# Attention kernel with inverses of the sums: from a rescaling of the output to a rescaling of the probabilities

## Chip, cores and metric

One core of one Trainium2 chip. The metric is the device time of one execution in microseconds (us); less is better.

## What is computed

x has shape (4, 1024, 1024): B = 4 batches, n = 1024 rows, dim = 1024, 16 heads of d = 64. With xn the RMS-normalised and modulated x and q, k RMS-normalised per head:

```python
qkv = xn @ W_qkv
logits = jnp.einsum('bhqd,bhkd->bhqk', q, k) * d ** (-0.5)
attn = jax.nn.softmax(logits, axis=-1)
o = jnp.einsum('bhqk,bhkd->bhqd', attn, v)
x = x + o + o @ W_out
x = x + causal_depthwise_conv(x, cond, b)
```

The change touches the softmax alone: where each row of exp(logits) is divided by its sum. All products run on pairs of half-precision numbers (a value and the rest that it leaves, "high" and "low"), so that every fp32 operand X is X_hi + X_lo, and a product takes three matmuls.

## The kernel before

A preparation scales and splits the weights (to about 204 us). Then come 32 **units** u, one per batch and pair of heads, each with eight **steps** p of 128 query rows. Each engine has its own program with the same loops, written by hand, and the engines meet by semaphores; each takes its instructions in order. Units differ in what they carry besides attention: units 0 to 30 project q, k, v of the next unit (`qkv`), units 0 to 23 prepare x of a later batch (`xs`), units 8 to 31 make output products of the batch before (`outs`), and units 9 to 31 also convolve and store (`fins`).

The work of one step, for the two heads h = 0, 1:

- PE: `score` (L723, 12 matmuls of 512 columns into the PSUM tensor `scores`). It first waits until the exps of the step before have read `scores` (`exp_done`). Behind it PE does half an `attend` (L742, probabilities times values, for two steps together), parts of the projection (L774), the output product (L798, L801) or transposes (L786, L811), by the step's number.
- VectorE (DVE): `maximum` of each head (L1178) and from it the exp's bias (L1181); then the step's other work, written between: x, convolution (L1266 to L1277), `normalise` (L1209, L1213), `sums` (L1198, L1201); then `low` of each head (L1187), the low half of the probabilities: prob minus its high half.
- ScalarE (ACT): exp of each head (L888) from PSUM into `prob`, with an accumulator read that gives the row sums `total`; then `high` of each head (L896), the copy to half precision; then copies for the other work.
- POOL: low halves of other operands; a DMA transposes each head's pair (L576) for `attend`.

VectorE starts the maxima of step p+1 only behind both `low` of step p. The exp of head h waits for `low` of the same head one step earlier, which frees `prob`.

**The inverses.** Two steps give four columns of sums, a group g. `invert` on VectorE (L1236, L1239, L1241) forms 1/sum and splits it in halves. `inverses` on PE (L757) transposes them, `inverse_rows` on ScalarE (L952) reads them to `inv_row`, a matmul with the constant `sel` (L749) spreads them over 64 rows a head, `read_inverses` (L958) reads that to `inv_all`, and `scale_values` on VectorE (L1250) multiplies: oT = values * inv_all. ScalarE makes its high half (`o_high`, L965) and POOL its low half (`o_lower`, L1131). PE's next `attend` waits for the inverse row (`inv_ev`).

## Time and profile before

| what | value |
|---|---|
| median of 3 runs | 2618.7 us (2618.64 to 2621.14) |
| profiled execution | 2618.81 us |
| its span | 2616.9 us |
| PE, VectorE, ScalarE, POOL busy | 91%, 80%, 69%, 25% of the span |
| TensorE clock granted, mean | 0.958 |

The profiled execution is as long as the median run; 1.9 us of it lie outside the span. Busy PE counts an engine whose matmuls are pipelined, so 91% is no statement on how much PE could lose: that is read by stretches and from the chain of waits. Where a view shows an idle time in brackets, it names the instruction that ended it.

### The profile page before, as it was taken

Reading aid. Unit: us, or ns where it says so; the run is one execution under the profiler, and the core shown is the slowest. Engines: PE = TensorE matmul, PEld = TensorE weight load, DVE = VectorE, ACT = ScalarE, POOL = GpSimd, SP = SyncE. Lnnn points to the kernel's source line nnn. Section 1 sums busy time; section 2 is a strip of 40 time slices with the busy share of each in tenths; the row PEclk is TensorE's granted clock in tenths of the full one; section 3 lists DMA queues with packets and bytes.
Section 4 is the critical chain, followed back from the end, with each engine's and each line's share of the span. In section 5 each row is a group of like instructions: output and inputs, shape, how many; then the busy total and the mean of one; then the engine's idle time right before and its main releaser. Section 6 shows DMA issues by size and latency. Waiting matters only on the chain.

```text
span 2616.9 us, 54024 instructions
## 1 busy us (share of the span) xinstructions
PE 2372.9 (91%) x20690; PEld 1527.4 (58%) x20690; DVE 2106.6 (80%) x3360; ACT 1815.4 (69%) x2823; POOL 660.5 (25%) x460
## 2 busy tenths in 40 slices
PE   1458998888889999999999999999999999999698
PEld 0034555555556666666666666666666666666487
DVE  6757777777778888888888888888888888888845
ACT  2237777777777877777777778777777777877611
POOL 0052322223222233222233232332222222222000
PEclk8879989989989999999999999999999999999789
DMA  6877988989999999999999999999988989887841
GB/s 236 344 192 152 172 166 174 180 173 179 218 197 183 185 203 184 193 190 219 205 206 193 200 187 189 196 186 229 193 176 171 179 162 182 165 164 155 158 150 61
DMA packets 1234881, 487.07 MB, mean 186 GB/s; under 512 B 1139521, under 2 KB 1196993, under 8 KB 1232065
## 3 DMA queue, kind: packets, MB, share of 16 engines
q1 hardware_dynamic: 1234624, 483.63, 87.8%
q8 instruction: 165, 2.70, 0.4%
q14 instruction: 92, 0.75, 0.1%
HBM read 141.13 MB, written 57.18 MB: 76 GB/s over the span
## 4 chain that ended last, share of the span: by engine, by line
PE 69%; DVE 11%; issue 6%; ACT 4%; SPq 3%; DMA 1%; POOL 0%; ACTq 0%; DVEq 0%
PE proj L774 36%; PE scores L723 11%; PE values L742 10%; PE proj L798 8%; DVE neg L1178 5%; DVE p_pair L1187 4%; SPq L576 3%; ACT p_pair L896 2%; PE proj L801 1%; PE misc L811 1%; DVE bias L1181 1%; ACT prob L888 1%; PE misc L786 1%; PE values L757 1%; PE values L749 1%
## 5 line engine op out<-in xcount | busy, mean ns | idle before, releaser
L774 PE MATMUL proj<-w_sb,xn_sb 128*128 128x384 f16 x6144 | 1029.4, 327 | 33.9 <-DMA xn_sb<-p_pair 29.1
L888 ACT ACTIVATE prob<-scores,bias,l_scale 128x1024 f32<-128x1024 f32 x512 | 615.5, 1203 | 353.7 <-DVE bias L1181 336.0
L774 PEld LDWEIGHTS proj<-w_sb,xn_sb 128*128 128x128 f16 x6144 | 588.9, 98 | 434.0 <-DMA xn_sb<-p_pair 25.6
L1178 DVE TENSOR_REDUCE neg<-scores 128x1 f32<-128x1024 f32 x512 | 623.8, 1218 | 156.1 <-PE scores L723 152.3
L1187 DVE TENSOR_TENSOR p_pair<-prob,p_pair 128x1024 f16<-128x1024 f32 x512 | 614.8, 1242 | 137.6 <-ACT p_pair L896 137.6
L896 ACT ACTIVATE p_pair<-prob 128x1024 f16<-128x1024 f32 x512 | 511.0, 1049 | 0.4 <-DMA pT<-p_pair 0.4
L723 PE MATMUL scores<-stack 64*128 64x512 f16 x3072 | 391.4, 389 | 58.8 <-ACT prob L888 57.1
L742 PE MATMUL values<-pT,v_pair 128*64 128x256 f16 x6144 | 396.9, 280 | 11.0 <-DMA pT<-p_pair 6.3
L742 PEld LDWEIGHTS values<-pT,v_pair 128*64 128x64 f16 x6144 | 324.2, 112 | 93.5 <-issue 78.6
L1102 POOL TENSOR_TENSOR rs<-ms,power 128x16 f32<-128x16 f32 x64 | 185.6, 2900 | 395.6 <-DVE ms L1201 395.6
L1131 POOL TENSOR_TENSOR oT_pair<-oT,oT_pair 128x256 f16<-128x256 f32 x128 | 148.7, 1162 | 541.4 <-ACT oT_pair L965 541.4
L723 PEld LDWEIGHTS scores<-stack 64*128 64x128 f16 x3072 | 131.7, 96 | 247.6 <-ACT prob L888 68.3
L798 PE MATMUL proj<-oT_in,wo 128*128 128x256 f16 x2304 | 267.7, 273 | 0.0
L798 PEld LDWEIGHTS proj<-oT_in,wo 128*128 128x128 f16 x2304 | 220.6, 98 | 30.0
L1107 POOL TENSOR_TENSOR qk_pair<-stage,qk_pair 128x512 f16<-128x512 f32 x128 | 146.7, 1167 | 329.8 <-ACT qk_pair L919 329.8
L1277 DVE SCALAR_TENSOR_TENSOR acc<-yT,taps,acc 128x256 f32<-128x256 f32 x384 | 186.2, 485 | 13.7
L952 ACT ACTIVATE inv_row<-values 4x256 f16<-4x256 f16 x128 | 47.1, 368 | 155.4 <-PE values L757 155.3
L904 ACT ACTIVATE stage<-proj 128x384 f32<-128x384 f32 x256 | 122.4, 478 | 31.4 <-PE proj L774 31.4
L1181 DVE TENSOR_SCALAR bias<-neg,l_scale 128x1 f32<-128x1 f32 x512 | 109.6, 214 | 18.0
L1127 POOL TENSOR_TENSOR pair<-x_in,pair 128x1024 f16<-128x1024 f32 x24 | 67.9, 2831 | 209.1 <-ACT pair L946 209.1
L232 PE MATMUL ps_row<-emb_w,smallT 128*4 128x512 f32 x64 | 40.4, 791 | 74.4 <-DMA emb_w<-in_L_cond_W_emb 74.4
L977 ACT ACTIVATE yT<-proj,y_now 128x512 f32<-128x512 f32 x64 | 43.8, 685 | 86.4 <-PE proj L801 70.2
(127 smaller groups left out, 2089.3 us busy)
## 6 DMA issues: line engine op xcount, KB each, us to landing
w_sb<-w_dram SPq DMA_DIRECT2D x128, 384.0 KB, 4.1
o_dram<-oT_pair SPq DMA_DIRECT2D x128, 128.0 KB, 2.5
out<-acc SPq DMA_DIRECT2D x64, 256.0 KB, 2.7
wq_raw<-in_L_cond_W_qkv SPq DMA_DIRECT2D x8, 1536.0 KB, 10.6
w_dram<-wq_pair SPq DMA_DIRECT2D x8, 1536.0 KB, 7.4
x_in<-in_x SPq DMA_DIRECT2D x24, 512.0 KB, 4.4
oT_in<-o_dram SPq DMA_DIRECT2D x12, 1024.0 KB, 6.0
xr<-in_x SPq DMA_DIRECT2D x24, 512.0 KB, 4.1
```

What stands on the lines that cost most here:

```text
L723: last = nc.tensor.matmul(scores[:, h, n * HN:(n + 1) * HN], stack[rows_, par, i, p * P:(p + 1) * P], stack[rows_, par, j, n * HN:(n + 1) ...
L742: last = nc.tensor.matmul(values[DH * h:DH * h + DH, 0:QG].rearrange("p (a n) -> p a n", a=2), v_pair[:, par, 2 * c + h, DH * i:DH * i + D ...
L774: last = nc.tensor.matmul(proj[:, t % 2, 0:6 * DH], xn_sb[:, t, i * K + c, :], w_sb[:, c, j, :], start=(c == 0 and i == j == 0), stop=(c = ...
L798: nc.tensor.matmul(dst, const["wo"][:, c, b, m * P:(m + 1) * P], oT_[:, c, a, :], start=(c == 0 and a == b == 0), stop=False)
L888: nc.scalar.activation(prob[:, h, :], scores[:, h, :], ACT.Exp, bias=bias[:, s:s + 1], scale=const["l_scale"][:, 0:1], accum_out=total[:, ...
L896: nc.scalar.activation(p_pair[:, s % 4, 0, :], prob[:, h, :], ACT.Copy).then_inc(hi_done, 1)
L1102: nc.gpsimd.tensor_tensor(rs[:], ms[:], const["power"][:, 0:4 * KH], ALU.pow).then_inc(h_pw, 1)
L1107: last = nc.gpsimd.tensor_tensor(qk_pair[:, j, 1].rearrange("p t (h d) -> p (t h) d", d=DH), stage[:, hf, :, j * DH:(j + 1) * DH], qk_pair ...
L1131: nc.gpsimd.tensor_tensor(oT_pair[:, 1], oT[:], oT_pair[:, 0], ALU.subtract).then_inc(o_low, 1)
L1178: nc.vector.tensor_reduce(neg[:, s:s + 1], scores[:, h, :], axis=AX.X, op=ALU.max, negate=True).then_inc(max_done, 1)
L1187: nc.vector.tensor_tensor(p_pair[:, s % 4, 1, :], prob[:, h, :], p_pair[:, s % 4, 0, :], ALU.subtract).then_inc(lo_done, 1)
L1277: nc.vector.scalar_tensor_tensor(out=acc[:, m, :], in0=yT[:, m, k:k + QG], scalar=const["taps"][:, k, c:c + 1], in1=acc[:, m, :], op0=ALU. ...
```

## The change

The probabilities themselves are divided by their sum, on the way to half precision. `high` becomes a copy of prob scaled by inv = 2^15 / sum, one number per row, read from memory, and `low` becomes prob * inv - high in one scalar_tensor_tensor. So `attend` gives the finished output (times 2^15), and the transposes on PE, `inv_row`, the product with `sel`, `inv_all` and the multiplication on VectorE go. `o_high` and `o_lower` read the PSUM tensor `values` themselves; `o_lower` moves from POOL to VectorE, at the place of `scale_values`, and `o_high` moves ahead of the two `high`, at the place of `read_inverses`. PE's next `attend` now waits for `o_low` of the group before. `invert` runs for every step instead of every second: a reciprocal and a multiplication by 2^15. In units 0 to 7 the first head is inverted right behind the maxima and the second behind the step's other work; in units 8 to 31 both behind the other work. The bias moves from VectorE to ScalarE (a copy of `neg` scaled by `l_scale`), ahead of each exp; its constant shift is dropped.

```diff
@@ PE
                 if part == 0:
-                    pe.wait_ge(inv_ev, n + 1)
+                    need(pe, o_low, n)
...
                 if part == 1:
                     last.then_inc(pv_done, 1)
-                    nc.tensor.matmul(values[:, QG:2 * QG], const["sel"][:], inv_row[:],
-                                     start=True, stop=True).then_inc(all_mm, 1)
-
-            def inverses(u, g):
-                n = NG * u + g
-                pe.wait_ge(inv_done, n + 1)
-                need(pe, o_done, n)
-                for a in range(2):
-                    last = nc.tensor.transpose(inv_bank[:, a * P:(a + 1) * P], inv_pair[:, g % 2, a, :],
-                                               const["eye16"][:])
-                last.then_inc(inv_tr, 1)
@@ ScalarE
             def exponent(u, p, h, par):
                 s = 2 * p + h
+                act.wait_ge(max_done, slot(u, s) + 1)
+                nc.scalar.activation(bias[:, s:s + 1], neg[:, s:s + 1], ACT.Copy,
+                                     scale=const["l_scale"][:, 0:1]).then_inc(bias_done, 1)
+                need(act, lo_done, slot(u, s) - 1)
                 act.wait_ge(bias_done, slot(u, s) + 1)
-                need(act, lo_done, slot(u, s) - 1)
-                if s % 4 == 0:
-                    need(act, inv_done, NG * u + s // 4 - 7)
+                if h == 0:
+                    need(act, inv_done, slot(u, s) - 2 * NS + 2)
...
             def high(u, p, h):
                 s = 2 * p + h
-                act.wait_ge(exp_done, slot(u, s) + 1)
+                act.wait_ge(inv_done, slot(u, s) + 1)
                 need(act, pT_in[(s + 4) % 8], 16 * (2 * u + (s + 4) // 8))
-                nc.scalar.activation(p_pair[:, s % 4, 0, :], prob[:, h, :], ACT.Copy).then_inc(hi_done, 1)
+                nc.scalar.activation(p_pair[:, s % 4, 0, :], prob[:, h, :], ACT.Copy,
+                                     scale=inv[:, p % 2, h:h + 1]).then_inc(hi_done, 1)
...
             def o_high(u, g):
                 n = NG * u + g
-                act.wait_ge(o_done, n + 1)
+                act.wait_ge(pv_done, n + 1)
                 need(act, o_st, 16 * n)
-                nc.scalar.activation(oT_pair[:, 0], oT[:], ACT.Copy).then_inc(o_hi, 1)
+                nc.scalar.activation(oT_pair[:, 0], values[:, 0:QG], ACT.Copy,
+                                     scale=1.0 / PROB_UP).then_inc(o_hi, 1)
@@ VectorE
             def maximum(u, p, h):
...
+                need(dve, bias_done, n - NS + 1)
                 nc.vector.tensor_reduce(neg[:, s:s + 1], scores[:, h, :], axis=AX.X, op=ALU.max,
                                         negate=True).then_inc(max_done, 1)
-                dve.wait_ge(max_done, n + 1)
-                nc.vector.tensor_scalar(bias[:, s:s + 1], neg[:, s:s + 1], const["l_scale"][:, 0:1], P_SHIFT,
-                                        ALU.mult, ALU.add).then_inc(bias_done, 1)
...
-                nc.vector.tensor_tensor(p_pair[:, s % 4, 1, :], prob[:, h, :], p_pair[:, s % 4, 0, :],
-                                        ALU.subtract).then_inc(lo_done, 1)
+                nc.vector.scalar_tensor_tensor(out=p_pair[:, s % 4, 1, :], in0=prob[:, h, :],
+                                               scalar=inv[:, p % 2, h:h + 1], in1=p_pair[:, s % 4, 0, :],
+                                               op0=ALU.mult, op1=ALU.subtract).then_inc(lo_done, 1)
...
+            def invert(u, p, par, h0, h1):
+                s = 2 * p
+                dve.wait_ge(exp_done, slot(u, s) + h1)
+                nc.vector.reciprocal(inv[:, p % 2, h0:h1], total[:, par * NS + s + h0:par * NS + s + h1]
+                                     ).then_inc(inv_rc, h1 - h0)
+                dve.wait_ge(inv_rc, slot(u, s) + h1)
+                nc.vector.tensor_scalar(inv[:, p % 2, h0:h1], inv[:, p % 2, h0:h1], PROB_UP, None,
+                                        ALU.mult).then_inc(inv_done, h1 - h0)
+
+            def o_lower(u, g):
+                dve.wait_ge(o_hi, NG * u + g + 1)
+                nc.vector.scalar_tensor_tensor(out=oT_pair[:, 1], in0=values[:, 0:QG], scalar=1.0 / PROB_UP,
+                                               in1=oT_pair[:, 0], op0=ALU.mult,
+                                               op1=ALU.subtract).then_inc(o_low, 1)
...
                 for p in range(K):
                     maximum(u, p, 0)
                     maximum(u, p, 1)
+                    if not outs:
+                        invert(u, p, par, 0, 1)
...
+                    invert(u, p, par, 0 if outs else 1, 2)
                     if p % 2 == 0 and p >= 4:
-                        scale_values(u, (p - 4) // 2)
+                        o_lower(u, (p - 4) // 2)
```

Where the instructions stand, VectorE in step 7 of a unit with output work, before (in brackets the semaphores that each waits for):

```order
L1178 TENSOR_REDUCE neg<-scores 128x1 [waits qk_done]
L1181 TENSOR_SCALAR bias<-neg,l_scale 128x1 [waits max_done]
L1178 TENSOR_REDUCE neg<-scores 128x1 [waits qk_done]
L1181 TENSOR_SCALAR bias<-neg,l_scale 128x1 [waits max_done]
L1266 TENSOR_SCALAR yT<-ends,carry 128x3 [waits halo,f_st0,y_ev]
L1270 TENSOR_SCALAR acc<-yT,taps,conv_b 128x256
L1273 COPY ends<-yT 128x3 [waits halo]
L1277 SCALAR_TENSOR_TENSOR acc<-yT,taps,acc 128x256 [waits cv,halo]
L1277 SCALAR_TENSOR_TENSOR acc<-yT,taps,acc 128x256 [waits cv] x2
L1187 TENSOR_TENSOR p_pair<-prob,p_pair 128x1024 [waits hi_done] x2
L1178 TENSOR_REDUCE neg<-scores 128x1 [waits qk_done]
```

and now:

```order
L1113 TENSOR_REDUCE neg<-scores 128x1 [waits bias_done,qk_done] x2
L1193 TENSOR_SCALAR yT<-ends,carry 128x3 [waits halo,f_st0,y_ev]
L1197 TENSOR_SCALAR acc<-yT,taps,conv_b 128x256
L1200 COPY ends<-yT 128x3 [waits halo]
L1204 SCALAR_TENSOR_TENSOR acc<-yT,taps,acc 128x256 [waits cv,halo]
L1204 SCALAR_TENSOR_TENSOR acc<-yT,taps,acc 128x256 [waits cv] x2
L1167 RECIPROCAL inv<-total 128x2 [waits exp_done]
L1170 TENSOR_SCALAR inv<-inv 128x2 [waits inv_rc]
L1119 SCALAR_TENSOR_TENSOR p_pair<-prob,inv,p_pair 128x1024 [waits hi_done] x2
L1113 TENSOR_REDUCE neg<-scores 128x1 [waits bias_done,qk_done] x2
```

The biases are gone; the reciprocal and its scaling stand behind the convolution and ahead of the two subtractions.

ScalarE in the same step 7, before:

```order
L952 ACTIVATE inv_row<-values 4x256 [waits all_mm,inv_tr]
L932 ACTIVATE stack<-misc 128x2x512 [waits h_tr]
L888 ACTIVATE prob,total<-scores,bias,l_scale 128x1024 [waits lo_done,bias_done] x2
L896 ACTIVATE p_pair<-prob 128x1024 [waits pT_in2,exp_done]
L896 ACTIVATE p_pair<-prob 128x1024 [waits pT_in3,exp_done]
L932 ACTIVATE stack<-proj 128x2x512 [waits h_tr]
L977 ACTIVATE yT<-proj,y_now 128x2x256 [waits cv,op_mm,y_set]
```

and now:

```order
L903 ACTIVATE stack<-misc 128x2x512 [waits h_tr]
L852 ACTIVATE bias<-neg,l_scale 128x1 [waits max_done]
L858 ACTIVATE prob,total<-scores,bias,l_scale 128x1024 [waits inv_done,bias_done,lo_done]
L852 ACTIVATE bias<-neg,l_scale 128x1 [waits max_done]
L858 ACTIVATE prob,total<-scores,bias,l_scale 128x1024 [waits bias_done,lo_done]
L866 ACTIVATE p_pair<-prob,inv 128x1024 [waits pT_in2,inv_done]
L866 ACTIVATE p_pair<-prob,inv 128x1024 [waits pT_in3,inv_done]
L903 ACTIVATE stack<-proj 128x2x512 [waits h_tr]
```

A bias stands ahead of each exp, the second one behind the first exp; the copies to `p_pair` wait for `inv_done` instead of `exp_done`; `inv_row` is gone.

VectorE in step 6 of a unit of the first kind (u = 0 to 7), now:

```order
L1113 TENSOR_REDUCE neg<-scores 128x1 [waits bias_done,qk_done] x2
L1167 RECIPROCAL inv<-total 128x1 [waits exp_done]
L1170 TENSOR_SCALAR inv<-inv 128x1 [waits inv_rc]
L1142 TENSOR_TENSOR stage<-stage,rs 128x8x128 [waits h_pw]
L1146 TENSOR_TENSOR stage<-stage,g_qk 128x8x64 [waits h_n]
L1167 RECIPROCAL inv<-total 128x1 [waits exp_done]
L1170 TENSOR_SCALAR inv<-inv 128x1 [waits inv_rc]
L1175 SCALAR_TENSOR_TENSOR oT_pair<-values,oT_pair 128x256 [waits o_hi]
L1119 SCALAR_TENSOR_TENSOR p_pair<-prob,inv,p_pair 128x1024 [waits hi_done] x2
```

The first head's inversion stands ahead of `normalise` (the two operations on `stage`), the second one behind it.

## Rows read from the trace of the kernel before

**Rows 1.** Page, part 1: busy time, share of the span, instructions

```profile
PE   2372.9 (91%) x20690; PEld 1527.4 (58%) x20690; DVE 2106.6 (80%) x3360; ACT 1815.4 (69%) x2823; POOL 660.5 (25%) x460
```

**Rows 2.** Windows: stretch, its length, busy us by engine, PEclk, DMA

```profile
471.50:542.20 70.70, 61.66 (x526) 36.45 (x528) 53.88 (x77) 52.21 (x83) 20.16 (x14) 0.91 0.87 172
...
1627.00:1698.60 71.60, 71.49 (x646) 46.85 (x647) 62.87 (x102) 56.10 (x89) 20.99 (x14) 1.00 0.96 199
```

**Rows 3.** Timeline, PE: first scores of units 8 and 31

```profile
764.10 2.03 PE L723 MATMUL scores<-stack 64*128 64x512 f16 x12
...
2415.04 1.47 PE L723 MATMUL scores<-stack 64*128 64x512 f16 x12
```

**Rows 4.** Chain of waits, units 20 and 21: start, length in us, what

```profile
1638.49 0.20 PE values L757 x2
...
1649.47 0.21 PE values L749
...
1685.21 1.45 PE scores L723 x12
...
1698.59 1.47 PE scores L723 x11
```

**Rows 5.** Timeline, DVE and ACT, step 7 of unit 19: start, length

```profile
1622.82 1.22 DVE L1178 TENSOR_REDUCE neg<-scores 128x1 f32<-128x1024 f32 x1
...
1624.32 1.20 ACT L888 ACTIVATE prob<-scores,bias,l_scale 128x1024 f32<-128x1024 f32 x1 [1.22 <-DVE bias L1181]
...
1625.70 1.20 ACT L888 ACTIVATE prob<-scores,bias,l_scale 128x1024 f32<-128x1024 f32 x1
...
1626.23 1.53 DVE L1277 SCALAR_TENSOR_TENSOR acc<-yT,taps,acc 128x256 f32<-128x256 f32 x3
...
1626.89 1.99 ACT L896 ACTIVATE p_pair<-prob 128x1024 f16<-128x1024 f32 x2
...
1627.97 2.36 DVE L1187 TENSOR_TENSOR p_pair<-prob,p_pair 128x1024 f16<-128x1024 f32 x2 [0.21 <-ACT p_pair L896]
...
1630.25 1.22 DVE L1178 TENSOR_REDUCE neg<-scores 128x1 f32<-128x1024 f32 x1
```

**Rows 6.** Groups by line and form: busy us, mean ns of one, idle before

```profile
L896 ACT ACTIVATE p_pair<-prob 128x1024 f16<-128x1024 f32 x512 | 511.0, 1049 | 0.4 <-DMA pT<-p_pair 0.4
...
L888 ACT ACTIVATION_READ_ACCUMULATOR prob<-scores,bias,l_scale 128x1 f32 x512 | 98.6, 193 | 0.0
...
L1209 DVE TENSOR_TENSOR stage<-stage,rs 128x1024 f32<-128x1024 f32 x64 | 78.0, 1218 | 6.0 <-POOL rs L1102 6.0
...
L919 ACT ACTIVATE qk_pair<-stage 128x512 f16<-128x512 f32 x128 | 73.5, 626 | 15.0 <-DVE stage L1213 15.0
...
L952 ACT ACTIVATE inv_row<-values 4x256 f16<-4x256 f16 x128 | 47.1, 368 | 155.4 <-PE values L757 155.3
...
L1236 DVE RECIPROCAL inv<-total 128x4 f32<-128x4 f32 x128 | 21.6, 169 | 0.0
...
L1224 DVE SCALAR_TENSOR_TENSOR pT<-pT,msx,rows 128x1024 f32<-128x1024 f32 x8 | 10.3, 1285 | 10.0 <-POOL msx L1122 10.0
...
L287 DVE SCALAR_TENSOR_TENSOR wo<-wo_raw,wo_top,wo 128x1024 f16<-128x1024 f32 x8 | 9.7, 1281 | 1.3 <-ACT wo L209 1.3
...
L209 ACT ACTIVATE wo<-wo_raw,wo_top 128x1024 f16<-128x1024 f32 x8 | 8.4, 1135 | 26.5 <-DVE wo_top L283 26.5
```

**Rows 7.** Timeline, units 19 and 20: step 5, and step 0's x

```profile
1604.94 1.22 DVE L1178 TENSOR_REDUCE neg<-scores 128x1 f32<-128x1024 f32 x1 [1.63 <-PE scores L723]
...
1607.36 1.20 ACT L888 ACTIVATE prob<-scores,bias,l_scale 128x1024 f32<-128x1024 f32 x1
...
1637.95 1.69 DVE L1224 SCALAR_TENSOR_TENSOR x_in<-x_in,msx,rows 128x1024 f32<-128x1024 f32 x1
```

**Rows 8.** Timeline, PE: waits in units of the first and second kind

```profile
542.18 2.74 PE L723 MATMUL scores<-stack 64*128 64x512 f16 x12 [4.32 <-ACT prob L888]
...
1275.41 4.07 PE L774 MATMUL proj<-w_sb,xn_sb 128*128 128x384 f16 x24 [3.01 <-DMA w_sb<-w_dram]
```

103 lines of the change are left out of this document (11 added, 92 removed).

## The prediction

> **What bounds the kernel now.** The page's first part says TensorE at 91% of the span, VectorE at 80% [rows 1]. That is an average; the stretches say more. The program has 32 units (u = 0 to 31). In a unit of the second kind (u = 8 to 31, with output work) PE is busy for 71.49 of 71.6 us, over the length of one of the first kind (u = 0 to 7) only for 61.66 of 70.7, partly at the lower clock [rows 2]. The 23 units 8 to 30 run from 764.10 to 2415.04, 71.8 us each [rows 3].
>
> The chain of waits through unit 20 shows who holds whom [rows 4]. From step 0 to step 5 it stays on PE, and the transposes of the inverses (0.20) and the product with sel (0.21) lie on it. At step 6's scores (1685.21) it leaves PE and runs through VectorE and ScalarE until the next unit's scores at 1698.59. So two things are nearly level in steps 6 and 7: PE's own work, which is unbroken there, and a ring of VectorE and ScalarE. The reader has to price that ring, not PE's share.
>
> The ring in step 7, its times counted in us from its first maximum at 1622.82 [rows 5]: first exp at +1.50, second exp at +2.88, first half-precision copy (L896) at +4.07, first subtraction (L1187) at +5.15, next step's first maximum at +7.43. VectorE takes its instructions in order, so the next maximum cannot pass the two subtractions; nothing else in the ring needs PE. In steps 0 to 5 PE's work takes 9 to 10 us a step and hides the ring.
>
> **What the change takes from PE.** Eight groups of instructions per unit, four of 0.20 and four of 0.21 us on the chain [rows 4]: 1.65 us. PE alone would need 71.55 - 1.65 = 69.9 us for a unit.
>
> **What it does to the ring.** Four edges change in every step.
> (a) The bias is made on ScalarE. The first costs there what it did on VectorE plus about 0.07. The second now stands behind the first exp and its accumulator read, no longer beside them. Its size, 128x1 with a scale read from memory, is not in the trace. Ends: 0.19, the accumulator read, and 0.37, a 4x256 copy [rows 6]. The copies of 1024 and of 512 columns (L896 1049 ns, L919 626) leave 0.20 for no columns at all, and a scale read from memory adds 0.08 to 0.09 (L209, the same copy with such a scale, 1135). I take 0.29, nearer to the first row, since nearly no columns are read. Then the exps start at +1.58 and +3.10 and the second sum is there at +4.39.
> (b) Units 8 to 31 invert both sums only after the second exp, and the copy now waits for this: reciprocal and scaling, 0.17 each [rows 6], with their hand-overs 0.43. The copy starts at +4.83, where it started at +4.07.
> (c) The copy reads its scale from memory: +0.09, by L209. The first subtraction starts at +6.00.
> (d) The subtraction becomes a scalar_tensor_tensor. L287 is that form at 1281 ns, a tensor_tensor of that size, L1209, 1218 [rows 6]: +0.06 twice. The turn closes at +8.40 instead of +7.43.
>
> The ScalarE price has a page: the Trainium skill, "ScalarE: Activation LUTs", section "What ACT_TABLE_LOAD costs", gives an ACTIVATE with constants 186 ns and each operand pointer about 93 ns more. By it the bias would be 0.28, not my 0.29, and the sum would hardly move; the trace agrees in the 86 ns between L209 and L896.
>
> **Other VectorE work in a turn.** The two biases leave VectorE (they held the next instruction up by 0.44 in all), so other work starts at +2.3. It delays the inversion only where it ends after +4.4. Per step, added to 8.40:
> step 0, x_multiply behind the subtractions: 1.7 today beside POOL's half of o (L1131) [rows 7], 1.28 at the start of the program, without it [rows 6]; POOL's piece is gone, so +1.2.
> step 1, convolution 2.2 (L1266 to the end of L1277 in rows 5) and x_shift 1.2, end +5.7: +1.2.
> step 2, convolution, in every second unit two small ones more: +0.2.
> step 3, convolution +0.1, and sums behind the subtractions, a reduction as long as L1209 and a small one: +1.55.
> step 4, normalise (L1209 and one of half its size, 1.9 together) cannot start before POOL's power of step 3's sums, +3.0, and ends at +4.95: +0.5.
> step 5, normalise behind the subtractions +1.9; and ScalarE comes late. Today its copies, projections, squares and output copy keep the first exp of step 5 until 1607.36, 2.4 us behind the maximum at 1604.94 where 1.5 is usual [rows 7]. The wait for the transposes before inv_row and a copy of o leave this queue, but step 4's copies start 0.9 later and step 5's maximum only 0.6: I put the lateness at 0.8: +2.7.
> step 6: 0. step 7: +0.1.
> Sum: 8 x 8.40 + 7.45 = 74.65 us. That exceeds PE's 69.9, so **the ring bounds all eight steps**, and PE waits 4.75 us: 1.4 before step 0's scores (a turn of 8.45 against 7.0 of PE work in step 7), the other 3.4 before step 7's.
>
> Could the chain mix both? It would leave the ring at step 7's second exp, run on PE through steps 0 to 5 and come back at step 6: 8.4 + 4.45 + (58.2 - 1.25) + 1.45 = 71.3 (58.2 is 71.55 less the 13.4 of steps 6 and 7 in rows 4). Less than 74.65, so it doesn't, as long as the ring's turns in steps 0 to 5 stand.
>
> **The sum.** Units 8 to 30: 23 x 74.65 = 1717, less 1.3 for unit 8, which has no convolutions in its steps 1 to 3, against 1650.9: +65. The short DMA waits in today's 71.8 vanish in PE's slack. Units 0 to 7 are written otherwise: the first sum is inverted right after the maxima, so the first copy doesn't wait. On the chain PE saves 1.03 in steps 0 to 4; the ring's steps 5 and 6 cost 0.23 and 0.43 more (bias, scaled copy, and the second inversion behind normalise). -0.4 each, -3 in all. Unit 31 is already short of PE work; eight turns at nearly +1: +7. The last products (2497 on) are untouched. VectorE's o_lower (128x256 from PSUM) stands where scale_values stood and lies beside the first copy; POOL's half of o and ScalarE's copies are hidden work on both sides: 0. Before the main part, one VectorE instruction less: -0.3.
> 2618.8 (profiled execution; the median is 2618.7, the same) + 65 - 3 + 7 = **2687 us**.
>
> **The rivals.**
> 1. The ring pays only in steps 6 and 7, and the answer is *faster*. In steps 0 to 5 PE's work of 9 to 10 us a step still hides the longer turns, and the chain is the mixed one above. It decides where the turns of steps 0 to 5 together come out over 3.4 us below mine. For it: the chain of before is on PE in those steps [rows 4]. Against: copy, inversion and subtraction are in series by their waits, and VectorE is in order. Time: 23 x 71.3 = 1640 (-11), units 0 to 7 -3 to -8, unit 31 +5: about 2610; if steps 6 and 7 were hidden too, 69.9 a unit and 2570. Chance 0.14.
> 2. All my small prices are too high (bias 0.19, scaled copy and new subtraction at today's durations): 0.4 less in each turn, 71.4 a unit, the time of before, 2610 to 2624. Chance 0.09, most of it within 0.2%.
> 3. The clock falls. Waits of 4.32 us before step 7 in the first units are followed by scores at half speed (2.74 for 1.47) [rows 8], and units 0 to 7 have a mean granted clock of 0.91 where the later ones have 1.00 [rows 2]. My forecast puts 3.4 us of wait there in each later unit. Step 7 has 7 us of PE work; slow for half or all of it costs 1.7 to 3.4, of which 1.4 plus a lead of 1.5 at the tightest step is covered: 0 to 2 us a unit, up to 2730. The Trainium skill, "TensorE: Matmul & The Clock Gate", section "HAM oscillation — how this bites in real kernels", tells of a kernel whose clock is throttled anew at each group of matmuls that follows a wait; by that rule this rival would be the case in all 23 units. In the trace it is so before step 7 of units 0 to 7. Against it here: PE is otherwise unbroken in the later units, and a wait of 3.01 us there (for w_sb, before 1275.41) kept matmuls of 0.17 us each, full speed [rows 8]. Chance 0.09.
>
> **How the numbers follow.** My forecast has 0.68; its own range is 2640 to 2715 (bias 0.37 adds 26, half of the cheap ends takes 40). A measurement of this kernel tells 0.2% (5 us) from no change. Faster by more: rival 1 and a part of 2, 0.16. Same: 0.07. Slower: 0.77. The range leaves out rival 1 and the far end of rival 3: 2615 to 2722.
>
> **What would show it.** Right: in units 8 to 30 the unit is 74 to 75 us; in step 7 the first copy starts 4.8 us after the first maximum and the next maximum 8.4 us after it; PE idles before the scores of steps 7 and 0, released by exp; the transposes and the sel product are gone; the bias takes near 0.29. Units 0 to 7 stay near 70. Wrong: units of 70 us with PE at 99%; a turn of 7.5 in step 7; or scores of 2.74 in the later units, which would be rival 3.

## The result, and the profile after

The changed kernel takes **2710.78 us** (median of 6 runs, 2709.11 to 2715.68); the kernel before, run beside it, 2622.03 (6 runs). The ratio is 1.0341, 95% interval 1.0325 to 1.0356: slower, as forecast. 2687 was forecast, with a range of 2615 to 2722. The profiled execution of the changed kernel took 2715.68 us and its span was 2713.8, 96.9 more than the span before. The medians lie 88.8 apart: this execution is 4.9 us above its median, the profiled one before 3.2 below the median of its six.

The page's first part for the changed kernel, beside [rows 1]:

```profile
PE 2331.5 (86%) x20306; PEld 1507.2 (56%) x20306; DVE 2015.0 (74%) x3103; ACT 1925.4 (71%) x3079; POOL 504.4 (19%) x332
```

PE does 41 us less work, VectorE 92 us less, ScalarE 110 us more, and the kernel is 97 us longer. Only ScalarE gained work, and at 71% it is not full either. The busy shares give no cause. The windows do a little better: unit 7, unit 20 and one of the later units (columns as in [rows 2]).

```profile
699.90:772.30 72.40, 60.25 (x514) 35.65 (x512) 52.94 (x80) 54.18 (x90) 15.79 (x10) 0.92 0.90 174
1678.98:1754.79 75.81, 70.20 (x634) 46.17 (x634) 58.76 (x89) 59.54 (x96) 15.57 (x10) 1.00 0.91 188
2056.50:2131.00 74.50, 69.92 (x634) 46.23 (x634) 56.32 (x84) 57.26 (x92) 12.58 (x8) 1.00 0.80 156
```

In unit 20 PE was busy for 71.49 of 71.6 us before; now it is busy for 70.20 of 75.81. It lost the expected work and got 5.6 us of waits. The clock stayed at 1.00, in unit 20 and, by windows of all of them, in each of the units 8 to 30. TensorE's timeline shows the first scores of unit 8 and the waits at step 7's scores and at the next unit's:

```profile
772.34 1.47 PE L706 MATMUL scores<-stack 64*128 64x512 f16 x12
...
1746.14 1.47 PE L706 MATMUL scores<-stack 64*128 64x512 f16 x12 [1.59 <-ACT prob L858]
...
1754.79 1.47 PE L706 MATMUL scores<-stack 64*128 64x512 f16 x12 [1.68 <-ACT prob L858]
```

PE waits for an exp, so it waits for the ring. No single wait in unit 20 is longer than these: the 5.6 us are 1.68, 0.82, 0.38, 0.98, 0.15 and 1.59, spread over steps 0, 1, 5, 6 and 7. Step 7 of unit 19 on VectorE and ScalarE answers to [rows 5]:

```profile
1674.43 2.35 DVE L1113 TENSOR_REDUCE neg<-scores 128x1 f32<-128x1024 f32 x2
...
1675.68 0.29 ACT L852 ACTIVATE bias<-neg,l_scale 128x1 f32<-128x1 f32 x1 [1.73 <-DVE neg L1113]
1676.05 1.21 ACT L858 ACTIVATE prob<-scores,bias,l_scale 128x1024 f32<-128x1024 f32 x1
1677.25 0.28 ACT L852 ACTIVATE bias<-neg,l_scale 128x1 f32<-128x1 f32 x1
1677.63 1.20 ACT L858 ACTIVATE prob<-scores,bias,l_scale 128x1024 f32<-128x1024 f32 x1
1678.73 0.19 ACT L858 ACTIVATION_READ_ACCUMULATOR prob<-scores,bias,l_scale 128x1 f32 x1
1679.02 0.17 DVE L1167 RECIPROCAL inv<-total 128x2 f32<-128x2 f32 x1 [0.16 <-ACT prob L858]
1679.29 0.17 DVE L1170 TENSOR_SCALAR inv<-inv 128x2 f32<-128x2 f32 x1
1679.50 2.19 ACT L866 ACTIVATE p_pair<-prob,inv 128x1024 f16<-128x1024 f32 x2 [0.58 <-DVE inv L1170]
1680.68 2.48 DVE L1119 SCALAR_TENSOR_TENSOR p_pair<-prob,inv,p_pair 128x1024 f16<-128x1024 f32 x2 [1.22 <-ACT p_pair L866]
1683.08 1.22 DVE L1113 TENSOR_REDUCE neg<-scores 128x1 f32<-128x1024 f32 x1
```

Counted from the first maximum at 1674.43: exps at +1.62 and +3.20 (forecast 1.58, 3.10), second sum ready at +4.49 (4.39), first copy at +5.07 (4.83), first subtraction at +6.25 (6.00), next maximum at +8.65 (8.40). Read the chain by its brackets: ScalarE's copy waited for the inverse, VectorE's subtraction for the copy, VectorE's reciprocal for the exp. Two engines at 59 us of work in a unit of 76 are each idle because of the other.

The groups by line and form: the bias, the scaled copy, the new subtraction, and x_multiply.

```profile
L852 ACT ACTIVATE bias<-neg,l_scale 128x1 f32<-128x1 f32 x512 | 147.2, 287 | 300.8 <-DVE neg L1113 298.9
L866 ACT ACTIVATE p_pair<-prob,inv 128x1024 f16<-128x1024 f32 x512 | 559.4, 1140 | 106.7 <-DVE inv L1170 106.7
L1119 DVE SCALAR_TENSOR_TENSOR p_pair<-prob,inv,p_pair 128x1024 f16<-128x1024 f32 x512 | 634.8, 1281 | 234.7 <-ACT p_pair L866 233.4
L1157 DVE SCALAR_TENSOR_TENSOR x_in<-x_in,msx,rows 128x1024 f32<-128x1024 f32 x24 | 30.7, 1277 | 0.0
```

The bias costs 287 ns (290 was taken), the copy 1140 against 1049 [rows 6], x_multiply 1277 where it took 1690 beside POOL [rows 7].

**Where the 96.9 us lie**, by the first scores of units 0, 8 and 31 in both traces (207.64, 772.34 and 2504.97 now): preparation +3.2 (forecast -0.3), units 0 to 7 +5.0 (-3), units 8 to 30 +81.7 (+65), unit 31 and the rest +7.0 (+7).

**Turns by step.** The same spacing (first maximum to first maximum, median over units 10 to 23; where even and odd units differ, as in step 5 with 11.30 and 11.41, the upper one) is the yardstick for every kernel below. The forecast stands under the measured turns of both kernels.

| step | 0 | 1 | 2 | 3 | 4 | 5 | 6 | 7 | sum |
|---|---|---|---|---|---|---|---|---|---|
| before | 9.32 | 8.52 | 9.97 | 8.99 | 9.44 | 10.17 | 7.71 | 7.43 | 71.55 |
| changed | 9.85 | 9.54 | 8.65 | 10.04 | 9.02 | 11.41 | 8.65 | 8.65 | 75.81 |
| forecast | 9.60 | 9.60 | 8.60 | 9.95 | 8.90 | 11.10 | 8.40 | 8.50 | 74.65 |

### The profile page after: what moved, and what is told of

It reads as the page before. It is cut to its first block and busy times, and to the rows that moved or that the text cites. A ratio compares the mean times of both kernels' runs of the same rounds, so it can differ in the third digit from the quotient of the medians.

```text
span 2713.8 us, 53370 instructions
## 1 busy us (share of the span) xinstructions
PE 2331.5 (86%) x20306; PEld 1507.2 (56%) x20306; DVE 2015.0 (74%) x3103; ACT 1925.4 (71%) x3079; POOL 504.4 (19%) x332
## 5 line engine op out<-in xcount | busy, mean ns | idle before, releaser
L1119 DVE SCALAR_TENSOR_TENSOR p_pair<-prob,inv,p_pair 128x1024 f16<-128x1024 f32 x512 | 634.8, 1281 | 234.7 <-ACT p_pair L866 233.4
L866 ACT ACTIVATE p_pair<-prob,inv 128x1024 f16<-128x1024 f32 x512 | 559.4, 1140 | 106.7 <-DVE inv L1170 106.7
L1113 DVE TENSOR_REDUCE neg<-scores 128x1 f32<-128x1024 f32 x512 | 601.1, 1215 | 36.1 <-PE scores L706 36.1
L852 ACT ACTIVATE bias<-neg,l_scale 128x1 f32<-128x1 f32 x512 | 147.2, 287 | 300.8 <-DVE neg L1113 298.9
L770 PE MATMUL proj<-oT_in,wo 128*128 128x256 f16 x2304 | 268.7, 273 | 21.1 <-ACT eye_x L929 10.4
L1167 DVE RECIPROCAL inv<-total 128x2 f32<-128x2 f32 (+1 forms) x320 | 52.2, 163 | 238.4 <-ACT prob L858 237.7
L875 ACT ACTIVATE stage<-proj 128x384 f32<-128x384 f32 x256 | 121.7, 476 | 71.6 <-PE proj L746 71.3
L1075 POOL TENSOR_TENSOR pair<-x_in,pair 128x1024 f16<-128x1024 f32 x24 | 58.4, 2435 | 362.6 <-ACT pair L917 362.6
L858 ACT ACTIVATION_READ_ACCUMULATOR prob<-scores,bias,l_scale 128x1 f32 x512 | 97.9, 191 | 0.0
## 6 DMA issues: line engine op xcount, KB each, us to landing
wq_raw<-in_L_cond_W_qkv SPq DMA_DIRECT2D x8, 1536.0 KB, 10.4
```

The source lines that it names most:

```text
L770: nc.tensor.matmul(dst, const["wo"][:, c, b, m * P:(m + 1) * P], oT_[:, c, a, :], start=(c == 0 and a == b == 0), stop=False)
L852: nc.scalar.activation(bias[:, s:s + 1], neg[:, s:s + 1], ACT.Copy, scale=const["l_scale"][:, 0:1]).then_inc(bias_done, 1)
L858: nc.scalar.activation(prob[:, h, :], scores[:, h, :], ACT.Exp, bias=bias[:, s:s + 1], scale=const["l_scale"][:, 0:1], accum_out=total[:, ...
L866: nc.scalar.activation(p_pair[:, s % 4, 0, :], prob[:, h, :], ACT.Copy, scale=inv[:, p % 2, h:h + 1]).then_inc(hi_done, 1)
L1113: nc.vector.tensor_reduce(neg[:, s:s + 1], scores[:, h, :], axis=AX.X, op=ALU.max, negate=True).then_inc(max_done, 1)
L1119: nc.vector.scalar_tensor_tensor(out=p_pair[:, s % 4, 1, :], in0=prob[:, h, :], scalar=inv[:, p % 2, h:h + 1], in1=p_pair[:, s % 4, 0, :], ...
```

## Experiments

Ten kernels. The theory: copy, inversion and subtraction now stand in series in a ring of VectorE and ScalarE, and this ring bounds all eight steps of units 8 to 31. The chief rival: the ring is paid for only in steps 6 and 7, and other things cost the time. Medians are of 4 to 6 runs; ratios are to the kernel before run on the same chip. Turns are medians over units 10 to 23.

| kernel | us | ratio (95%) | units 0-7 | units 8-30 | turns 0, 1, ... 7 |
|---|---|---|---|---|---|
| e1 bias back on VectorE | 2701.15 | 1.0308 (1.0291-1.0325) | 556.5 | 1728.0 | 9.59 10.03 9.13 10.29 9.02 10.65 8.39 8.90 |
| e2 first sum inverted early | 2655.56 | 1.0134 (1.0119-1.0150) | 564.1 | 1677.0 | 9.43 9.27 9.52 9.53 8.48 10.47 8.24 8.13 |
| e3 no factor 2^15 | 2673.40 | 1.0205 (1.0190-1.0221) | 562.1 | 1693.4 | 9.57 9.26 8.52 9.77 8.75 11.13 8.38 8.37 |
| e4 inverse of the step before | 2630.16 | 1.0032 (1.0020-1.0044) | 564.4 | 1651.8 | 9.44 8.22 9.56 9.36 8.65 10.31 8.24 7.97 |
| e5 before, bias on ScalarE | 2651.89 | 1.0120 (1.0105-1.0135) | 568.1 | 1676.3 | 9.64 8.06 9.97 9.16 9.27 10.79 8.02 7.76 |
| e6 other VectorE work moved | 2664.13 | 1.0158 (1.0143-1.0174) | 563.8 | 1687.5 | 8.65 8.65 9.72 8.79 9.23 10.85 8.65 8.65 |
| e7 e6 and e3 together | 2643.14 | 1.0079 (1.0064-1.0094) | 563.8 | 1666.0 | 8.38 8.88 9.76 8.79 9.22 10.30 8.38 8.37 |
| e8 e7, parts taken back | 2632.75 | 1.0044 (1.0030-1.0059) | 559.9 | 1666.3 | 8.38 8.88 9.76 8.79 9.23 10.29 7.98 8.63 |
| e9 before, scaled forms | 2639.61 | 1.0070 (1.0053-1.0087) | 567.1 | 1664.0 | 9.53 8.51 9.97 9.04 9.39 10.22 7.92 7.64 |
| e10 e8, early inversion in 4 steps | 2606.14 | 0.9944 (0.9931-0.9958) | 557.6 | 1641.4 | 8.23 9.15 9.76 8.79 9.22 9.97 7.98 7.71 |

### The two small prices alone: e9

```diff
@@ before: high, low
-                nc.scalar.activation(p_pair[:, s % 4, 0, :], prob[:, h, :], ACT.Copy).then_inc(hi_done, 1)
+                nc.scalar.activation(p_pair[:, s % 4, 0, :], prob[:, h, :], ACT.Copy,
+                                     scale=one[:, 0:1]).then_inc(hi_done, 1)
-                nc.vector.tensor_tensor(p_pair[:, s % 4, 1, :], prob[:, h, :], p_pair[:, s % 4, 0, :],
-                                        ALU.subtract).then_inc(lo_done, 1)
+                nc.vector.scalar_tensor_tensor(out=p_pair[:, s % 4, 1, :], in0=prob[:, h, :],
+                                               scalar=one[:, 0:1], in1=p_pair[:, s % 4, 0, :],
+                                               op0=ALU.mult, op1=ALU.subtract).then_inc(lo_done, 1)
```

> The kernel before with the half-precision copy scaled by a 1 read from memory and the subtraction as a scalar_tensor_tensor with the same 1: the two small prices (c) and (d) alone, no change of waits. By the prediction's prices, a turn of the ring grows by 0.09 + 2 x 0.06, about 0.2 us, of which only steps 6 and 7 are paid, 0.4 us a unit: 2629 to 2633 us. Rival (these forms are free): 2621. Rival (dearer in their place): over 2640.

Measured 2639.61. The forms cost what was forecast, as the groups show (before: 1049 and 1242 ns a piece):

```profile
L896 ACT ACTIVATE p_pair<-prob,one 128x1024 f16<-128x1024 f32 x512 | 557.9, 1141 | 0.0
L1188 DVE SCALAR_TENSOR_TENSOR p_pair<-prob,one,p_pair 128x1024 f16<-128x1024 f32 x512 | 644.4, 1300 | 150.3 <-ACT p_pair L896 150.3
```

Turns 6 and 7 each grew by 0.21, exactly the 0.2 of edges (c) and (d). But turn 0 grew by 0.21 too, so a unit costs 0.68 instead of 0.4: in the kernel before three turns are paid for, not two. And units 0 to 7 lost 7.4 us. With these two the expected band, 2629 to 2633, was missed by 7 us, though both prices were right. A fifth of a microsecond in this ring is 17 us in the kernel.

### The bias on ScalarE alone: e5 and e1

e5 is the kernel before with the bias as the change makes it; the constant shift that the bias carried is dropped, and the later scaling is set to fit.

```diff
@@ before: exponent, maximum
-                act.wait_ge(bias_done, slot(u, s) + 1)
+                act.wait_ge(max_done, slot(u, s) + 1)
+                nc.scalar.activation(bias[:, s:s + 1], neg[:, s:s + 1], ACT.Copy,
+                                     scale=const["l_scale"][:, 0:1]).then_inc(bias_done, 1)
...
-                nc.vector.tensor_scalar(bias[:, s:s + 1], neg[:, s:s + 1], const["l_scale"][:, 0:1], P_SHIFT,
-                                        ALU.mult, ALU.add).then_inc(bias_done, 1)
```

> The kernel before with the bias alone moved to ScalarE, its shift dropped (and the inverses scaled by 2^10 instead of 2^22). Theory: PE hides the ring in steps 0 to 5, so only steps 6 and 7 pay 0.3 each: +0.6 to 0.7 a unit, 2632 to 2642. Rival (the bias on ScalarE is what costs): +60 to +90, near 2700.

Measured 2651.89, above the expected band: +31. Step 7 of unit 19 shows where it is paid. The second bias stands behind the first exp's accumulator read; the copies follow at once:

```profile
1638.71 0.29 ACT L885 ACTIVATE bias<-neg,l_scale 128x1 f32<-128x1 f32 x1 [1.15 <-DVE neg L1182]
1639.10 1.21 ACT L891 ACTIVATE prob<-scores,bias,l_scale 128x1024 f32<-128x1024 f32 x1
1640.20 0.19 ACT L891 ACTIVATION_READ_ACCUMULATOR prob<-scores,bias,l_scale 128x1 f32 x1
1640.30 0.28 ACT L885 ACTIVATE bias<-neg,l_scale 128x1 f32<-128x1 f32 x1
1640.67 1.21 ACT L891 ACTIVATE prob<-scores,bias,l_scale 128x1024 f32<-128x1024 f32 x1
1641.78 0.19 ACT L891 ACTIVATION_READ_ACCUMULATOR prob<-scores,bias,l_scale 128x1 f32 x1
1641.87 1.99 ACT L899 ACTIVATE p_pair<-prob 128x1024 f16<-128x1024 f32 x2
```

From bias start to exp start it is 0.37 to 0.39 for an instruction of 0.28: 0.09 or so of hand-over on the same engine, twice. Turns 6 and 7 rose by 0.31 and 0.33, a unit by 1.12, and units 0 to 7 by 8.4 us in all. The other half of the 1.12 lies in turns that the expectation took for hidden: 0 (+0.32), 3 (+0.17) and 5 (+0.62), less 0.46 in turn 1 and 0.17 in turn 4.

e1 takes the same part out of the changed kernel.

```diff
@@ after: exponent, maximum
-                act.wait_ge(max_done, slot(u, s) + 1)
-                nc.scalar.activation(bias[:, s:s + 1], neg[:, s:s + 1], ACT.Copy,
-                                     scale=const["l_scale"][:, 0:1]).then_inc(bias_done, 1)
...
+                dve.wait_ge(max_done, n + 1)
+                nc.vector.tensor_scalar(bias[:, s:s + 1], neg[:, s:s + 1], const["l_scale"][:, 0:1], 0.0,
+                                        ALU.mult, ALU.add).then_inc(bias_done, 1)
```

> The changed kernel with the bias back on VectorE (without its constant shift). Theory (the ring VectorE-ScalarE bounds units 8 to 30, and its loss is the inversion between second exp and first copy): the second exp starts 0.3 earlier, so turns without other VectorE work shrink by 0.3 (steps 0, 5, 6), but other work on VectorE starts 0.45 later, and where it ends behind the second exp the inversion moves with it (steps 1, 2, 3, 7: +0.25 to +0.45). Sum +0.4 us a unit, in all 2705 to 2722. Rival (the bias on ScalarE is what costs, 0.3 in each of eight turns): -2.4 us a unit, near 2655.

Measured 2701.15, some 10 us less than the changed kernel, and 8.2 of them lie in units 0 to 7 (556.5 against 564.7). The band of 2705 to 2722 was missed by 4 us: it said nothing of units 0 to 7, and put +0.4 on a unit, where units 9 to 23 stayed as they were and units 24 to 30 lost 0.6 each. In the later units the bias has two signs. In turn 6, where VectorE has nothing else, it costs 0.26 on ScalarE (8.65 against 8.39). In turn 7, where the convolution stands ahead of the inversion, it gains 0.25 (8.65 against 8.90), because VectorE reaches the inversion earlier:

```profile
1664.71 1.53 DVE L1203 SCALAR_TENSOR_TENSOR acc<-yT,taps,acc 128x256 f32<-128x256 f32 x3
1666.15 0.16 DVE L1166 RECIPROCAL inv<-total 128x2 f32<-128x2 f32 x1
1666.42 0.17 DVE L1169 TENSOR_SCALAR inv<-inv 128x2 f32<-128x2 f32 x1
```

That reciprocal starts at +4.85 after the first maximum (1661.30), and without a wait: VectorE itself was late. In the changed kernel it is at +4.59, and ends a wait of 0.16 for the exp.

### The series itself: e2, e3, e4

e2 inverts the first head's sum right behind the maxima in units 8 to 31 too:

```diff
-                    if not outs:
-                        invert(u, p, par, 0, 1)
+                    invert(u, p, par, 0, 1)
...
-                    invert(u, p, par, 0 if outs else 1, 2)
+                    invert(u, p, par, 1, 2)
```

> The changed kernel with units 8 to 31 inverting as units 0 to 7 do: first head right behind the maxima, second head behind the other work. Theory: the first copy no longer waits for the inversion; turns of steps 5 and 4 shrink by 0.7, of 0 and 6 by 0.4, of 3 and 7 by 0.15 (there the other work now starts 1 us later), 1 and 2 stay. -2.35 us a unit, near 2657. Rival (the loss is in durations: scaled copy, scalar_tensor_tensor, bias): no change, 2711.

Measured 2655.56, as the theory had it. The same instructions are executed and more of them (VectorE does 61.06 us in unit 20 instead of 58.76), and 55 us are gone. Its step 7 of unit 19, first maximum at 1643.22:

```profile
1646.18 0.16 DVE L1167 RECIPROCAL inv<-total 128x1 f32<-128x1 f32 x1 [0.61 <-ACT prob L858]
...
1647.62 1.14 ACT L866 ACTIVATE p_pair<-prob,inv 128x1024 f16<-128x1024 f32 x1
1648.97 1.15 ACT L866 ACTIVATE p_pair<-prob,inv 128x1024 f16<-128x1024 f32 x1 [0.21 <-DVE inv L1170]
```

The first copy now follows the second exp directly, at +4.40 instead of +5.07. VectorE pays for it with an idle 0.61 ahead of the convolution, and it is still a gain, 0.52 in that turn. The only turn that is longer is step 2's (9.52 against 8.65). It has little other work, and by then PE's own matmuls are what the ring waits for (below, e6).

e3 leaves the factor 2^15 out of the probabilities and of the output's scaling (`PROB_UP` is 1, and the multiplication and its wait go):

```diff
-                                     ).then_inc(inv_rc, h1 - h0)
-                dve.wait_ge(inv_rc, slot(u, s) + h1)
-                nc.vector.tensor_scalar(inv[:, p % 2, h0:h1], inv[:, p % 2, h0:h1], PROB_UP, None,
-                                        ALU.mult).then_inc(inv_done, h1 - h0)
+                                     ).then_inc(inv_done, h1 - h0)
```

> The changed kernel without the multiplication by 2^15: inv is the plain reciprocal, and the reads of the output are not scaled down. It leaves out this scaling alone. Theory: one VectorE operation and its hand-over, 0.27 us, leave the ring in each of the eight turns: -2.15 us a unit, near 2660. Rival (PE or the durations bound the unit): no change, 2711.

Measured 2673.40: 37 us for one VectorE instruction of 0.17 us a step. Turns without other work shrink by 0.27, the spacing of reciprocal and multiplication in the changed kernel's timeline (1679.02 to 1679.29). That is 13 us short of the 50 expected. In units 10 to 23 it gave 2.06 of the 2.16 a unit (turn 2 only 0.13), but in units 24 to 30 only 1.35 (74.80 to 73.45): there turn 1 grew from 8.65 to 8.89 and turn 2 from 9.72 to 9.76. What holds those two is not the ring but PE: the maxima at the ends of both wait for PE's scores (0.42 and 1.30 us in unit 25).

e4 keeps every instruction and takes the wait alone away: copy and subtraction use the inverse of the step before, which is ready (so each row is divided by another step's sum).

```diff
-                act.wait_ge(inv_done, slot(u, s) + 1)
+                act.wait_ge(exp_done, slot(u, s) + 1)
+                need(act, inv_done, slot(u, 2 * p))
...
-                                     scale=inv[:, p % 2, h:h + 1]).then_inc(hi_done, 1)
+                                     scale=inv[:, (p + 1) % 2, h:h + 1]).then_inc(hi_done, 1)
```

> The changed kernel, whose scaled copy and subtraction use the inverse of the step before (each row is divided by another step's sum), so that the first copy waits only for the first exp and no longer for the second exp and the inversion. Every instruction of the changed kernel is still there. Theory (the copy's wait for the inversion is what lengthens the turns of VectorE and ScalarE): the turns shrink by 0.4 to 1.1 us each, about 5 us in a unit, down to where the chain through TensorE's own work takes over, 71.3 to 71.4 us a unit; 2600 to 2615 us. Rival (the added instructions, not the wait, cost the time): units stay above 75 us and the time near 2710.

Measured 2630.16: 80 of the 89 are gone. This is the experiment that settles the main question, for the added work is all there and only the wait isn't. The unit is 71.75 long and, by the windows, PE is busy for 70.02 of it. Seven of the eight turns are 0.4 to 1.3 us shorter than in the changed kernel; turn 2 is 0.9 longer, since VectorE then waits for PE's scores. The unit is 0.4 us longer than the 71.3 to 71.4 that the mixed chain gave, which is 9 of the 15 us by which it missed its band; the other 6 are units 15 and 23, which took 74.98 and 74.78 and in the changed kernel 75.9 and 75.5, next to nothing above their neighbours. There PE waits for weights, and the slower ring had hidden it.

### Where VectorE's other work stands: e6, e7

```diff
@@ after: VectorE, unit
+                        if outs:
+                            x_multiply(v, par, x_in[:])
...
-                        if xs:
+                        if xs and not outs:
                             x_shift(v, x_in[:])
...
+                    if outs and xs and p == 1:
+                        x_shift(v, x_in[:])
+                    if outs and qkv and p == 3:
+                        sums(w, 0)
...
-                    if p == 0 and xs:
+                    if p == 0 and xs and not outs:
...
-                    if p == 3 and qkv:
+                    if p == 3 and qkv and not outs:
```

> The changed kernel with VectorE's other work of units 8 to 31 put elsewhere: x_multiply (step 0) ahead of the inversion, x_shift (step 1) right behind it, sums (step 3) between inversion and subtractions, where VectorE stands idle and waits for ScalarE. Nothing is added or taken out. Theory (VectorE's order within the turns of steps 0, 1 and 3 puts 1.2 to 1.6 us of its other work on the ring, and the ring bounds all eight steps): 3.75 us less in each of units 8 to 23, 1.65 less in the later ones, about 2640 us. Rival (TensorE bounds steps 0 to 5, only 6 and 7 are paid): no change, near 2710.

Measured 2664.13: the direction is the theory's, 47 us from moving three operations into idle time, and the rival's "no change" is out. The size is short of 70. Turn by turn against the changed kernel: -1.20, -0.89, **+1.07**, -1.25, +0.21, -0.56, 0, 0. What was saved in steps 0 and 1 came back in step 2, at 9.72. Steps 2 and 3 take 9.72 and 8.79 here, 9.76 and 8.79 in e7, e8 and e10: they are PE's own work in those steps, the 9.97 and 8.99 of the kernel before less one 0.20 each. So in the changed kernel PE was about 1.1 us ahead at step 2, and the saving of one turn is kept only as far as PE's work allows. In units 24 to 30, which have no x work and where 1.65 was expected, the unit went from 74.80 to 73.20, 1.60.

> The kernel of e6 without the factor 2^15: one VectorE instruction and one wait less between the second exp's sum and the first copy in every step. If the ring still bounded everything the two gains would add (37 + 70 us, to about 2604); but by the theory the mixed chain (ring in steps 6 and 7, TensorE in steps 0 to 5) stands at about 71.5 us a unit and takes over: about 2620, the time of the kernel before.

Measured 2643.14, above both numbers, 23 us over the theory's. The gains don't add (47 and 37 became 68), as the mixed chain says, but its floor was put too low, 71.5 against 72.08 (13 us in 23 units). Units 15 and 23, at 76.7 and 76.5, stand 9 us above their neighbours. The forecast chain came back to the ring at step 6. VectorE's timeline of e6 shows that it comes back a step earlier. The last wait for PE in the unit is the one before step 5's maximum:

```profile
1694.95 2.36 DVE L1113 TENSOR_REDUCE neg<-scores 128x1 f32<-128x1024 f32 x2 [0.48 <-PE scores L706]
...
1703.94 1.22 DVE L1142 TENSOR_TENSOR stage<-stage,rs 128x1024 f32<-128x1024 f32 x1
1705.19 0.69 DVE L1146 TENSOR_TENSOR stage<-stage,g_qk 128x512 f32<-128x512 f32 x1
1705.80 2.35 DVE L1113 TENSOR_REDUCE neg<-scores 128x1 f32<-128x1024 f32 x2
```

From 1694.95 on the ring is what is paid. It takes 10.85 in step 5, since `normalise` (1.86, L1142 and L1146) stands between the subtractions and step 6's maximum, where it was before too, and since ScalarE is late with step 5's first bias (1696.54, 1.59 after the start of the maximum, where 1.25 is usual). The mixed chain has to be priced with turn 5 on the ring.

The other part of e6's shortfall: 1.13 a unit over 16 units is 18 us, and unit 23 took 77.4 us, 4 more than its neighbours: PE waits 2.82 us for weights, and the 24 matmuls behind it take 5.57 instead of 4.07, at a lower clock.

### A version that beats both: e8, e10

e8 adds to e7: bias on VectorE in units 0 to 7 and in steps 6 and 7, and the first sum inverted early in step 6.

```diff
+                if u < K or p >= 6:
+                    dve.wait_ge(max_done, n + 1)
+                    nc.vector.tensor_scalar(bias[:, s:s + 1], neg[:, s:s + 1], const["l_scale"][:, 0:1], 0.0,
+                                            ALU.mult, ALU.add).then_inc(bias_done, 1)
...
-                    if not outs:
+                    if not outs or p == 6:
                         invert(u, p, par, 0, 1)
```

> The kernel of e7 (no factor 2^15, VectorE's other work put where it waits) with two parts of the change taken back where the ring is what is paid for: the bias on VectorE in units 0 to 7 and in steps 6 and 7 of the later ones, and in step 6 the first sum inverted right behind the maxima. Theory (ring and TensorE's work share the unit by steps, and what is paid is the turns of steps 5 to 7, 0 and 1): units of 70.8 to 71.6 us, units 0 to 7 at 557, in all 2598 to 2622 us, at or under the time of the kernel before. Rival (something else has taken over and e7's 72.08 us is its floor): 2635 to 2645.

Measured 2632.75, outside the theory's 2598 to 2622 and near the rival's band. Not for the rival's reason: turn 6 did fall, 8.38 to 7.98, but turn 7 rose, 8.37 to 8.63. It is what e1 had shown in turn 7: with the bias on VectorE the convolution ends later, and the unsplit inversion stands behind it. I had put a part into a turn where its measured sign is the wrong one. Units 15 and 23 took 78.7 and 78.0 us as well, 13 us above their neighbours in all (in the changed kernel there was nothing of that): waits for weights of 4.64 and 3.98 us, and the 24 matmuls behind them took 6.95 and 5.75 instead of 4.07, so 4.6 of the 13 are the clock's. So units 8 to 30 gained nothing on e7 (1666.3 against 1666.0), and units 0 to 7 gained 3.9. So e10 puts the first inversion ahead of the convolution in step 7 too, and in steps 0 and 5:

```diff
-                    if not outs or p == 6:
+                    if not outs or p in (0, 5, 6, 7):
...
-                    invert(u, p, par, 0 if outs and p != 6 else 1, 2)
+                    invert(u, p, par, 0 if outs and p not in (0, 5, 6, 7) else 1, 2)
```

> The kernel of e8 with the first sum inverted right behind the maxima in steps 0, 5, 6 and 7 of units 8 to 31, so that the first copy of these steps doesn't wait for the second exp. e2 showed 0.4 us less in a turn without other VectorE work, 0.5 in step 7 and 0.9 in step 5, with the factor still in. Theory: another 0.5 to 1.0 us a unit below e8, down to at least the 69.9 us of TensorE's own work: about 12 to 24 us below e8's time, and faster than the kernel before by over 0.2%. Rival (TensorE is the bound already in e8): e8's time, and TensorE busy for over 99% of a unit.

Measured **2606.14**, ratio 0.9944 (0.9931 to 0.9958) to the kernel before: the one version that is faster, by 0.56%. It is 26.6 us below e8, a little over the 12 to 24 expected, and a unit lost 1.13 us where 0.5 to 1.0 was expected, 0.92 of it in turn 7. The page's first part and unit 20 by the windows:

```profile
PE 2323.4 (89%) x20306; PEld 1506.6 (58%) x20306; DVE 2043.0 (78%) x3103; ACT 1866.0 (72%) x2855; POOL 526.4 (20%) x332
...
1617.60:1688.40 70.80, 69.76 (x632) 46.20 (x632) 59.51 (x90) 58.20 (x93) 16.53 (x10) 1.00 0.98 201
```

70.80 a unit against 69.76 of PE work: of the 1.65 us that the change takes from PE, 0.75 are now seen. Less of it reaches the whole: units 15 and 23 take 76.2 and 77.6, since PE waits there for weights, longer than before (3.01 in [rows 8]):

```profile
1841.05 5.76 PE L746 MATMUL proj<-w_sb,xn_sb 128*128 128x384 f16 x24 [4.79 <-DMA w_sb<-w_dram]
```

## Why the prediction was right, and where it was off

**Right: the mechanism.** A ring of VectorE and ScalarE, not PE, bounds the changed kernel in units 9 to 23, and in units 24 to 30 in all steps but step 2; copy, inversion and subtraction in series make its turns longer; PE's saving of 1.65 us a unit turns into waits. Taking away the wait alone gives back 80 of 89 us (e4), and inverting one sum earlier 55 (e2). Rival 1 (the ring pays only in steps 6 and 7) is out: e6 changes only steps 0, 1 and 3, and gains 47 us. Rival 2 is out by durations. Rival 3 didn't come about: the clock is 1.00 in all of the units 8 to 30.

**Where PE waits.** The sum was near (5.6 us for 4.75), the places were not. Forecast were 1.4 before step 0's scores and 3.4 before step 7's; measured were 1.68 and 1.59, with the rest in small pieces before the projection and the output products. So the long wait on which rival 3 rested never arose, and the changed kernel doesn't show whether the argument against that rival was sound (e4 and e10, in the last section, have longer waits, with and without the clock's fall). Nor does that rival's price come out of its own row: 2.74 for 1.47 puts 3.0 to 6.0 us on half or all of 7 us of matmuls, where 1.7 to 3.4 was written.

**Edge (a), bias on ScalarE.** Its duration was right (0.287 for 0.29). What was mis-sized is the hand-over: exp starts 0.37 to 0.38 after the bias starts, where 0.29 plus 0.03 had been put for it. The exps came at +1.62 and +3.20 instead of +1.58 and +3.10: 0.10. The rule of the Trainium skill that stood there ("ScalarE: Activation LUTs", section "What ACT_TABLE_LOAD costs") gives 0.28 for the instruction, and the trace agrees with 0.287; the hand-over stands on top of it.

**Edge (b), the inversion.** Forecast 0.43 from second sum to copy, measured 0.58 (1678.92 to 1679.50): 0.10 before the reciprocal, 0.27 from its start to the multiplication's, 0.21 to the copy. The term was mis-sized by 0.15. Together with (a) that is the whole of the turn's 8.65 against 8.40.

**Edges (c), (d).** Right: e9 measures 0.21 a turn for 0.2.

**The additions by step.** Over a turn of 8.65 they are 1.20, 0.89, 0.00, 1.39, 0.37, 2.76, 0 and 0, in all 6.61 for the forecast 7.45 (1.2, 1.2, 0.2, 1.55, 0.5, 2.7, 0, 0.1). Turns +2.0, additions -0.84: 75.8 for 74.65. Step 1 was taken too high because the inversion behind x_shift started at +5.5 (1698.41 against the maximum at 1692.92; 5.7 forecast) and couldn't have started before +4.6 anyway (4.4 forecast). "8 x 8.40 + 7.45" was charged to all 23 units, though units 24 to 30 have no x work in steps 0 and 1. They measured 74.5 to 75.2 all the same, because PE's own work holds their step 2 at 9.72: two omissions that cancel, which was luck. So the term for units 8 to 30, +65, came out at +81.7 mainly through units 9 to 23, at 75.5 to 76.2.

**Units 0 to 7.** This is the step that failed in sign: -3 forecast, +5.0 measured. By median turns over units 2 to 6, PE saved 1.01 in steps 0 to 4, as forecast (1.03): 46.92 and 45.91 in all. But the ring's steps were priced at 0.23 and 0.43 more in steps 5 and 6, and turns 5, 6 and 7 rose from 7.66, 7.71 and 8.37 to 8.09, 8.24 and 8.91, by 1.50. The hand-overs of the bias were missing, and that step 7 pays too. So there is no gain left: by the first scores, units 1 to 5 together take what they took before (352.9 us), where 2 less was forecast. The +5.0 itself lies in three units: unit 0 +1.75 (its turns 0 and 1 were 8.64 and 7.43 before, not the 9.97 and 8.99 of PE's work in later units, so the ring is paid there too: +0.42 and +0.55), unit 6 +1.55, and unit 7 +1.78. In unit 7 PE waits for weights, which it didn't before:

```profile
707.54 4.07 PE L746 MATMUL proj<-w_sb,xn_sb 128*128 128x384 f16 x24 [1.34 <-DMA w_sb<-w_dram]
```

The same turn (step 0 of unit 7, 11.27 for 9.97) is 11.1 to 11.4 in e1, e3 and e7 as well. Unit 6's excess is a turn 7 of 9.67, which is 7.97 in e3 and e7 and 8.91 in e1, so it may belong to this one execution. e1, with the bias back on VectorE, has 556.5 us in units 0 to 7, -3.2 to the kernel before. That is the forecast's number, but not its path: units 1 to 6 became 4.5 us shorter and unit 7 became 1.5 longer.

**The mixed chain** (71.3) was not needed for the number, but e4, e6 and e7 tested it: 71.75 in e4, where it was nearly right, and 73.20 and 72.08 in e6 and e7 where it should have been 71.8 and 71.5. It returned to the ring at step 6; the runs show that it does so in step 5, behind `normalise`.

**Preparation** (+3.2 for -0.3) was not studied. In e1, e2, e3, e4, e6 and e7, whose preparation is the changed kernel's or nearly so, the first scores stand at 203.2 to 206.2 (204.4 before, 207.6 in the changed kernel), so most of it may be spread between executions.

## What to carry to other kernels

When PE shows 91% and its chain is unbroken, taking work from it pays only as far as the next ring of engines allows; find that ring in the timeline, count its turn from one start to the next, and price every edit in turns. Here 0.1 us a turn is 256 turns, up to 25 us. A dependence that is moved from a side path (the inverses behind the output) into a ring is paid in turn after turn, however small the instruction (without this one, in e4, seven of eight turns were 0.4 to 1.3 us shorter); whether an engine's other work stands ahead of or behind the waited-for instruction was worth more than half of what the change cost (47 and 55 of 89 us). Take an instruction's effect with its sign in each turn: the same bias on the same engine cost 0.26 in one and gained 0.25 in the next.
